# Two-layer graph block on one Trainium2 core: first layer as A(xW) in place of (Ax)W, its early sums stored as a finished node table

## Chip, core and metric

One core of a Trainium2 chip. The metric is device time in microseconds (us). The engines are TensorE (PE), VectorE (DVE), ScalarE (ACT), GpSimd (POOL) and SyncE (SP, which here only issues DMAs).

## What is computed

3125 nodes with 256 features each, 103125 edges sorted by destination (16 relation types). A is the matrix of edge counts with self loops, dinv the inverse root of the degree.

```python
def conv(h, W, b):
    h = h @ W
    agg = segment_sum(h[src] * norm, dst, num_segments=n)   # norm = dinv[src] * dinv[dst]
    return agg + b
h = relu(layernorm(x))
h = relu(conv(h, W1, b1)); h = relu(conv(h, W2, b2)); x = x + conv(h, W3, b3)
h = relu(layernorm(x))
red = segment_sum(h[src] + relvectors[edge_type], dst)       # without self loops
x = x + gru_cell(red, h, w_ih, w_hh, b_ih, b_hh)
```

## The kernel before

It never gathers rows. It first **builds** A as a dense f16 matrix of counts (`count`, 25 tiles of 128 sources by 3125 destinations), and then every layer is a chain of matmuls over it. All node tables are held as two f16 parts, high and low (the low part is the value minus the high part), so each product is two matmuls.

**The build** runs over 202 windows of 512 edges. For two windows at a time (a pair), DVE makes one-hot matrices (`one_hot`, L740, "hot"), into two buffers that take turns, and for pair m it waits until PE has done window 2m-3. PE multiplies them in a PSUM bank (L677, with small matmuls L682, L691, L693), ACT copies the window's 20 columns into `count` (L863). The banks form a ring of 6.

**Beats.** Each engine has four beats of side work per window, numbered 0, 1, 2, ... by constants (`VARIANCE_AT`, `DEGREE_AT`, ...). DVE does beats 8m to 8m+7 behind the one-hots of pair m, ACT beats 4s to 4s+3 behind its copy of window s, PE beats 4(s-1) to 4s-1 behind window s. Before the change they hold: the counts per rank for the degrees (L701, beats 0 to 19, PE), statistics of x (L441), degrees (L710, one burst behind window 9), the roots, and from beat 60 the table of the first layer: DVE shapes a tile of x (`L849`), ACT takes its high part (L873), DVE its low part (L840).

**Early products** (L731). From window 24 PE adds products of the first layer to every window, 1000 in all, each with a tile of the table stationary and 256 columns of `count` moving: `units` of 256 destinations that are already complete (`settled`), each in two halves of the features. They give (Ax) transposed for the first 2560 destinations. ACT copies each half out of PSUM (L882), SP stores it in DRAM (`table_scratch`). GpSimd adds the identity to the diagonal of each unit (L747).

**Behind the build** (`layers_pe`): SP loads the weights and the stored sums. PE makes the sums for the last 565 destinations (L915, 512 and 53 columns moving), and between them `conv_pe` (L929) multiplies the sums of all 25 tiles by W1, in f32. `scale_pe`, `scale_dve` and `scale_act` take the largest column sums of the weights, from which the powers of two that scale the f16 tables come. DVE (L1058, L1068, L1062) and ACT (L1133) make the table of the second layer, `node_b`, from the results. Then come layers 2 and 3 (700 products each), and the last with the GRU.

## Time and profile before

| | |
|---|---|
| median of 3 runs | 981.91 us (981.41 to 982.49) |
| the profiled execution | 982.03 us, of which its span 978.1 us |
| busy | PE 904.8 us, DVE 498.8, ACT 268.0, POOL 11.1 |
| matmuls on PE | 6312 |

The span is what lies between the first and the last instruction. Busy times overlap, since the engines run beside each other. PE is busy for 93% of the span, but it is so for different reasons in different stretches, so the stretches count and not the sum.

### The profile page before, as it was taken

The numbers are of one execution on the slowest core, as the hardware profiler recorded it, in microseconds if no ns is written. First come the engines' busy times: TensorE is split into PE (matmuls) and PEld (weight loads), VectorE is DVE, ScalarE is ACT, GpSimd is POOL, SyncE is SP. The second block draws the span as 40 slices with busy tenths as digits, with TensorE's granted clock in tenths as the row PEclk, the third lists the DMA queues.
The fourth block names the chain that finished last, engine by engine and source line by source line (L and its number), as shares of the span: only waits on it lengthen the run. The fifth ranks groups of instructions, "written<-read, shape, count | busy, mean of one in ns | idle before, by whom it ended". The sixth has DMA issues, their size and how long they took to land.

```text
span 978.1 us, 15791 instructions
## 1 busy us (share of the span) xinstructions
PE 904.8 (93%) x6312; PEld 557.3 (57%) x6312; DVE 498.8 (51%) x1300; ACT 268.0 (27%) x518; POOL 11.1 (1%) x18
## 2 busy tenths in 40 slices
PE   1654999999999798999999999999999999999996
PEld 1533888888888465544445454444455455555553
DVE  7999888888888164101112152333615133333435
ACT  3143444555544221101111120222322112122222
POOL 0000000000000000000000000000000000000000
PEclk9985999999999999999999999999999999999999
DMA  6000000000000400000000010111131000010010
GB/s 183 1 1 1 13 13 13 13 12 12 18 12 13 151 0 13 1 0 1 1 1 1 22 47 24 39 43 38 54 114 41 8 21 22 25 30 21 22 33 30
DMA packets 24502, 27.13 MB, mean 28 GB/s; under 512 B 2785, under 2 KB 22413, under 8 KB 24424
## 3 DMA queue, kind: packets, MB, share of 16 engines
q1 hardware_dynamic: 23752, 25.65, 8.3%
q8 instruction: 52, 0.85, 0.4%
q10 hardware_dynamic: 672, 0.41, 0.2%
q14 instruction: 26, 0.21, 0.1%
HBM read 17.03 MB, written 9.02 MB: 27 GB/s over the span
## 4 chain that ended last, share of the span: by engine, by line
PE 86%; DVE 10%; DMA 1%; ACT 1%; issue 1%; SPq 1%; DVEq 0%; ACTq 0%
PE ps L915 41%; PE ps L731 12%; PE ps L677 10%; PE ps L550 9%; PE ps L929 7%; PE ps L554 4%; DVE node_b L740 2%; DVE node_a L840 1%; PE ps L682 1%; DVE count L441 1%; PE ps L693 1%; DMA params<-in_L_gnn_b 1%; PE ps L535 1%; DVE count L797 1%; DVE agg L849 1%
## 5 line engine op out<-in xcount | busy, mean ns | idle before, releaser
L915 PE MATMUL ps<-count,node_b 128*128 128x512 f16 (+3 forms) x1400 | 271.3, 351 | 0.7 <-DVE node_b L1128 0.7
L740 DVE TENSOR_TENSOR node_b<-node_b 128x50 f16<-128x50 f16 (+4 forms) x455 | 208.6, 524 | 16.3 <-PE ps L677 16.3
L677 PE MATMUL ps<-node_b 128*128 128x225 f16 (+1 forms) x808 | 172.2, 298 | 35.5 <-DVE node_b L740 35.4
L915 PEld LDWEIGHTS ps<-count,node_b 128*128 128x128 f16 (+2 forms) x1400 | 121.4, 98 | 142.9 <-issue 8.4
L863 ACT ACTIVATE count<-ps 128x500 f32 x202 | 123.2, 610 | 164.6 <-PE ps L677 164.5
L915 PE MATMUL ps<-count,node_a 128*128 128x512 f16 (+1 forms) x900 | 162.6, 338 | 5.8 <-DMA params<-in_L_gnn_W 5.8
L731 PE MATMUL ps<-count,node_a 128*128 128x256 f16 (+1 forms) x1000 | 143.0, 274 | 0.0
L915 PEld LDWEIGHTS ps<-count,node_a 128*128 128x128 f16 x900 | 72.7, 98 | 93.2 <-issue 15.8
L677 PEld LDWEIGHTS ps<-node_b 128*128 128x128 f16 x808 | 83.1, 104 | 46.3 <-DVE node_b L740 34.4
L731 PEld LDWEIGHTS ps<-count,node_a 128*128 128x128 f16 (+1 forms) x1000 | 95.5, 98 | 20.8 <-issue 6.9
L682 PE MATMUL ps<-node_b,params 128*128 128x9 f16 (+1 forms) x808 | 104.7, 177 | 0.0
L1058 DVE SCALAR_TENSOR_TENSOR work<-ps,dinv,params 128x256 f32<-128x256 f32 (+1 forms) x50 | 24.0, 480 | 133.2 <-PE ps L929 110.5
L682 PEld LDWEIGHTS ps<-node_b,params 128*128 128x128 f16 x808 | 82.1, 102 | 11.1
L570 DVE TENSOR_TENSOR node_a<-ps,node_a 128x512 f32<-128x512 f32 (+1 forms) x25 | 17.2, 689 | 94.5 <-PE ps L550 94.5
L1137 ACT ACTIVATE agg<-ps,scales 128x512 f32<-128x512 f32 (+1 forms) x36 | 22.8, 638 | 120.4 <-PE ps L915 120.4
L929 PE MATMUL ps<-params,agg 128*128 128x256 f32 (+1 forms) x220 | 51.6, 386 | 4.2 <-ACT agg L1137 4.2
L1108 DVE SCALAR_TENSOR_TENSOR work<-ps,dinv,params 128x256 f32<-128x256 f32 (+1 forms) x25 | 12.1, 484 | 80.0 <-PE ps L929 79.3
L929 PEld LDWEIGHTS ps<-params,agg 128*128 128x128 f32 (+1 forms) x220 | 39.7, 186 | 14.9 <-ACT agg L1137 5.4
L550 PE MATMUL ps<-node_a 128*128 128x512 f32 (+1 forms) x100 | 47.0, 592 | 0.0
L512 ACT ACTIVATE node_a<-ps 128x256 f32<-128x256 f32 (+1 forms) x25 | 9.5, 378 | 125.3 <-PE ps L535 125.3
L693 PE MATMUL ps<-node_b 128*128 128x25 f16 x201 | 37.5, 186 | 0.0
L550 PE MATMUL ps<-node_a,agg 128*128 128x512 f32 x64 | 30.7, 601 | 2.6 <-issue 2.1
(195 smaller groups left out, 692.9 us busy)
## 6 DMA issues: line engine op xcount, KB each, us to landing
node_a<-in_x SPq DMA_DIRECT2D x4, 768.0 KB, 7.5
table_scratch<-agg SPq DMA_DIRECT2D x20, 128.0 KB, 1.8
node_b<-table_scratch SPq DMA_DIRECT2D x5, 512.0 KB, 8.6
xt<-x_scratch SPq DMA_DIRECT2D x16, 128.0 KB, 2.2
out<-scaled SPq DMA_DIRECT2D x16, 128.0 KB, 1.7
xt<-in_x SPq DMA_DIRECT2D x12, 128.0 KB, 2.1
params<-in_x SPq DMA_DIRECT2D x12, 128.0 KB, 2.1
x_scratch<-xt SPq DMA_DIRECT2D x12, 128.0 KB, 1.7
```

The lines of the kernel that those rows point to most:

```text
L550: done = PE.matmul(ps[0:m, rz, 0:2 * D], l, w[:, f, 0:2 * D], start=(n == 0), stop=(n == 2 * HALVES - 1))
L554: done = PE.matmul(ps[0:m, nn, col:col + D], ls[f], w[:, f, 2 * D:G], start=(f == 0), stop=(f == HALVES - 1))
L677: return PE.matmul(window(s)[:, :, first:first + n], low, key_hot[k][j // 2][:, j % 2, :, i].rearrange("p (t w) -> p t w", w=n), start=(s ...
L682: PE.matmul(ps[:, s % RING, last_tile + first:last_tile + first + n], rel_window(g, s % SMALL, j), span_hot[g][:, s % SMALL * QUARTERS // ...
L693: PE.matmul(window(s + 1)[:, :, 0], low, carry_hot[k][:, :, i], start=False, stop=False, skip_group_check=True)
L731: last = PE.matmul(ps[:, 6 + f, 0:UNIT], node_a[0:k, t, part, f * P:(f + 1) * P], count[0:k, t, u * UNIT:(u + 1) * UNIT], start=(t == 0 an ...
L740: return DVE.tensor_tensor(to, iota, keys.unsqueeze(2).to_broadcast([P, n, width, 2]), ALU.is_equal)
L863: ACTE.activation(to, window(s), ACT.Copy).then_inc(win_written, 1)
L915: last = PE.matmul(ps[:, b, 0:cols], nodes[0:k, t, part, f * P:(f + 1) * P], count[0:k, t, c * CHUNK:c * CHUNK + cols], start=(n == 0 and ...
L929: done = PE.matmul(ps[0:m, b, 0:D], sums[:, f, at_col:at_col + m], weight[i % 2][:, f, :], start=(f == 0), stop=(f == HALVES - 1))
L1058: DVE.scalar_tensor_tensor(out=work[k][0:m, :], in0=ps[0:m, 4 + (first + n) % 4, 0:D], scalar=dinv[0:m, t:t + 1], in1=bias[layer][0:m, :], ...
L1137: ACTE.activation(to[:, 0:cols], ps[:, h % AGG_RING, 0:cols], ACT.Copy, scale=inverse_scale).then_inc(sums_out, 1)
```

## The change

**The order of the first layer.** relu(layernorm(x)) W1 is made before the neighbours are summed. rstd is positive, so relu(rstd (x - mean)) is rstd relu(x - mean), and rstd is applied behind W1. GpSimd centres each tile of x as 2x minus twice its mean (L1333). PE turns the tile (two f32 transposes, one each beat from beat 8), ACT copies it back with Relu, PE multiplies it by W1 in f32 (three beats later), ACT copies that back over the tile (`beside_pe`, `beside_act`). There is one PSUM bank for the turned tile and one for the weighted one. From beat 58 ACT makes the high part of the table straight from it with the factor as scale (L1025), and DVE the low part from beat 68 (L905), so that DVE no longer shapes it. The table lies three tiles further down in the memory (`table0`), so ACT may write tile t only when DVE has made tile t-3.

**The early products** have the tile of `count` stationary and 256 features of the table moving: 128 destinations at once with all their features, 50 products for a tile of destinations, 21 tiles (1050 products). The first two are made together, 16 products a window from window 20, the other 950 from window 29 to the end. The result is the first layer's output itself. DVE adds the bias (L959), ACT does relu, scale and the high part (L967, L971), DVE the low part (L976), and SP stores the finished tile in DRAM, all during the build; four DMAs bring 21 tiles back to `node_b`.

**Moved and removed.** The scales are computed in the build (beats 37, 49 to 55). Behind the build PE makes 200 products of 256 columns for the last four tiles, with no `conv_pe` for the first layer, no `scale_pe` and no wait for the weights. The ring has 5 banks (L677 waits for `win_written` of one window less). GpSimd adds the diagonal by tiles of 128, 21 times.

```diff
-RING = 6
-EARLY = 5
+RING = 5
+EARLY = 21
+SHIFT = 3
...
+        TURN_AT = 8
+        WEIGH_AT = TURN_AT + 3
+        COLUMNS_AT = WEIGH_AT + T + 1
+        SCALE_AT = 49
+        FACTORS_AT = 58
+        LOW_PART_AT = FACTORS_AT + 10
+        OUT_AT, OUT_LOW_AT = 5, 9
...
+        PAIR_FROM = (LOW_PART_AT + 3) // BEATS + 3
+        REST_FROM = 29
+        early_products = [(u, t, part) for t in range(T) for u in range(2) for part in range(2)]
+        pair_products = len(early_products)
+        early_products += [(u, t, part) for u in range(2, EARLY) for t in range(T) for part in range(2)]
...
+        def beside_pe(beat):
...
+            t = beat - TURN_AT
+            if 0 <= t < T:
+                m = rows(t)
+                PE.wait_ge(x_centred, t + 1)
+                if t:
+                    PE.wait_ge(x_turned_out, t)
+                for f in range(HALVES):
+                    last = PE.transpose(TURNED[:, f, 0:m], h1[0:m, t, f * P:(f + 1) * P], ident[0:m, 0:m])
+                last.then_inc(x_turned, 1)
+            t = beat - WEIGH_AT
+            if 0 <= t < T:
+                m = rows(t)
+                PE.wait_ge(x_turned_out, t + 1)
+                PE.wait_ge(*((x_weighted_out, t) if t else (w_early_in[0], 16)))
+                for f in range(HALVES):
+                    last = PE.matmul(WEIGHED[0:m, :], turned_x(t)[:, f, 0:m], w_early[0][:, f, :], start=(f == 0), stop=(f == HALVES - 1))
+                last.then_inc(x_weighted, 1)
...
+            last = PE.matmul(out_slot(u)[0:m, :], count[0:k, t, u * P:u * P + m], table0(t)[0:k, part, :],
+                             start=(t == 0 and part == 0), stop=(t == T - 1 and part == 1), skip_group_check=True)
             if t == T - 1 and part == 1:
-                last.then_inc(early_summed, 1)
+                last.then_inc(conv_done, 1)
...
+        def out_bias_dve(u):
+            m, k = rows(u), u % 2
+            DVE.wait_ge(conv_done, u + 1)
...
+            DVE.scalar_tensor_tensor(out=work[k][0:m, :], in0=out_slot(u)[0:m, :], scalar=newt[0:m, 1, u:u + 1], in1=xt[1][0:m, :],
+                                     op0=ALU.mult, op1=ALU.add).then_inc(conv_read, 1)
...
+            t = beat - TURN_AT
+            if 0 <= t < T:
+                m = rows(t)
+                ACTE.wait_ge(x_turned, t + 1)
+                ACTE.activation(turned_x(t)[:, :, 0:m], TURNED[:, :, 0:m], ACT.Relu).then_inc(x_turned_out, 1)
+            t = beat - WEIGH_AT
+            if 0 <= t < T:
+                m = rows(t)
+                ACTE.wait_ge(x_weighted, t + 1)
+                ACTE.activation(h1[0:m, t, :], WEIGHED[0:m, :], ACT.Copy).then_inc(x_weighted_out, 1)
...
         def fast_pool():
+            for t in range(T):
+                m = rows(t)
+                POOL.wait_ge(x_summed, min(t // 6, XG) + 1)
+                POOL.tensor_scalar(h1[0:m, t, :], h1[0:m, t, :], 2.0, moments[0:m, t, 0:1], ALU.mult, ALU.subtract).then_inc(x_centred, 1)
```

PE's instructions at the end of window 4, where two of its four beats can be seen. L701 (L738 after) are the counts per rank, L749 the transposes, L757 the product with W1, "waits" are the semaphores. Before:

```order
L693 MATMUL ps<-node_b 128x25
L677 MATMUL ps<-node_b 128x25x11
L701 MATMUL ps<-ones,count 128x1 [waits ranks_ready]
L701 MATMUL ps<-ones,count 128x1 x3
L701 MATMUL ps<-ones,count 74x1 x4
```

Now:

```order
L697 MATMUL ps<-node_b 128x25x11
L738 MATMUL ps<-ones,count 128x1 [waits ranks_ready]
L738 MATMUL ps<-ones,count 128x1 x3
L738 MATMUL ps<-ones,count 74x1 x4
L749 MATMUL ps<-ident,node_a 128x128 [waits x_turned_out,x_centred]
L749 MATMUL ps<-ident,node_a 128x128
L757 MATMUL ps<-count,node_a 128x256 [waits x_weighted_out,x_turned_out]
L757 MATMUL ps<-count,node_a 128x256
```

Each beat from 11 to 32 has a transpose pair and a product pair on PE now, and both wait for a copy by ACT.

PE's instructions where the build ends: the last early products (L731, now L779), and what follows. Before:

```order
L731 MATMUL ps<-count,node_a 128x256 x5
L915 MATMUL ps<-count,node_a 128x512 [waits w0_in,w1_in,chunk_looped,win_written]
L915 MATMUL ps<-count,node_a 128x512 x25
L938 MATMUL ps<-agg,xt 128x256 [waits abs_made]
L938 MATMUL ps<-agg,xt 128x256 x3
L915 MATMUL ps<-count,node_a 128x512 x12
L929 MATMUL ps<-params,node_b 128x256 [waits early_in0]
```

Now:

```order
L779 MATMUL ps<-node_a,count 128x256 x5
L1095 MATMUL ps<-scaled,count 128x256 [waits conv_read,chunk_looped,win_written]
L1095 MATMUL ps<-scaled,count 128x256 x3
L1095 MATMUL ps<-xt,count 128x256 x2
L1095 MATMUL ps<-node_a,count 128x256 x44
L1095 MATMUL ps<-scaled,count 128x256 [waits conv_read]
```

The waits for the weights and the stored sums are gone from this place, and so are L938 and L929.

DVE's instructions between the one-hots of two pairs (windows 18 and 19) in the table's stretch. Before:

```order
L740 TENSOR_TENSOR node_b<-node_b 128x1100
L840 SCALAR_TENSOR_TENSOR node_a<-scaled,node_a 128x256 [waits table_high]
L849 TENSOR_SCALAR scaled<-node_a,newt 128x256 [waits table_ready]
L840 SCALAR_TENSOR_TENSOR node_a<-scaled,node_a 128x256 [waits table_high]
L849 TENSOR_SCALAR scaled<-node_a,newt 128x256 [waits table_ready]
L840 SCALAR_TENSOR_TENSOR node_a<-work,node_a 128x256 [waits table_high]
L849 TENSOR_SCALAR work<-node_a,newt 128x256 [waits table_ready]
```

Now:

```order
L788 TENSOR_TENSOR node_b<-node_b 128x50
L788 TENSOR_TENSOR node_b<-node_b 128x1100
L905 SCALAR_TENSOR_TENSOR node_a<-node_a,newt 128x256 [waits table_high] x8
L788 TENSOR_TENSOR params<-node_b 128x8x32 [waits win_done]
L788 TENSOR_TENSOR node_b<-node_b 128x1024
```

Of the two operations for a tile one is left, in runs of eight.

## Rows read from the trace of the kernel before

**Rows 1.** Windows: stretch, length, busy us of PE, PEld, DVE, ACT, POOL; PEclk; DMA

```profile
24.00:60.50 36.50, 24.78 (x336) 19.95 (x335) 35.77 (x108) 9.14 (x16) 0.00 (x0) 1.00 0.01 2
60.50:92.50 32.00, 11.90 (x109) 7.73 (x108) 31.14 (x86) 15.04 (x37) 0.67 (x1) 0.56 0.00 1
92.50:322.30 229.80, 229.74 (x2778) 195.22 (x2776) 191.03 (x439) 113.39 (x198) 7.91 (x9) 0.99 0.04 13
322.30:381.80 59.50, 50.32 (x309) 32.72 (x310) 30.83 (x87) 13.71 (x35) 0.38 (x1) 0.97 0.20 63
```

**Rows 2.** Timeline of ACT (start, us): copies of windows 10, 11, 13, 14 and 28

```profile
57.87 0.59 ACT L863 ACTIVATE count<-ps 128x500 f32 x1 [2.75 <-PE ps L677]
58.97 0.60 ACT L863 ACTIVATE count<-ps 128x500 f32 x1 [0.51 <-PE ps L677]
61.22 0.60 ACT L863 ACTIVATE count<-ps 128x500 f32 x1 [0.17 <-PE ps L677]
62.01 0.59 ACT L863 ACTIVATE count<-ps 128x500 f32 x1 [0.19 <-PE ps L677]
...
99.55 0.59 ACT L863 ACTIVATE count<-ps 128x500 f32 x1 [0.71 <-PE ps L677]
```

**Rows 3.** Timeline of PE: the rank counts behind window 3, the start of window 10

```profile
35.27 1.77 PE L701 MATMUL ps<-ones,count 128*128 128x1 f16 x32
56.47 0.39 PE L677 MATMUL ps<-node_b 128*128 128x225 f16 x1 [1.00 <-DVE node_b L740]
```

**Rows 4.** Timeline in the GRU: a transpose pair, the next matmul, ACT's copy

```profile
817.22 0.38 PE L535 MATMUL ps<-ident,scaled 128*128 128x128 f32 x2
817.44 1.89 PE L915 MATMUL ps<-count,node_b 128*128 128x512 f16 x8
817.64 0.38 ACT L512 ACTIVATE node_a<-ps 128x256 f32<-128x256 f32 x1 [4.14 <-PE ps L535]
```

**Rows 5.** Timeline behind the build: four tiles by W1, the next matmul, DVE

```profile
340.37 3.62 PE L929 MATMUL ps<-params,node_b 128*128 128x256 f32 x16
343.82 2.86 PE L915 MATMUL ps<-count,node_a 128*128 128x512 f16 x12
344.09 0.48 DVE L1058 SCALAR_TENSOR_TENSOR work<-ps,dinv,params 128x256 f32<-128x256 f32 x1 [2.20 <-PE ps L929]
```

**Rows 6.** Timeline: a copy by ACT and the PE matmul that waits for it

```profile
373.83 0.58 ACT L1137 ACTIVATE agg<-ps 128x512 f32<-128x512 f32 x1
374.46 3.72 PE L929 MATMUL ps<-params,agg 128*128 128x256 f32 x16 [1.41 <-ACT agg L1137]
```

**Rows 7.** Timeline of ACT: the load of the table for Sqrt

```profile
49.39 1.28 ACT L421 ACT_TABLE_LOAD   x1
```

**Rows 8.** Timeline: one-hots beside a GpSimd operation, the operation, one-hots alone

```profile
108.43 2.60 DVE L740 TENSOR_TENSOR node_b<-node_b 128x176 f16<-128x176 f16 x5 [0.32 <-PE ps L677]
109.18 1.17 POOL L747 TENSOR_TENSOR count<-count,ident 128x256 f16<-128x256 f16 x1 [33.70 <-ACT count L863]
113.52 2.13 DVE L740 TENSOR_TENSOR node_b<-node_b 128x176 f16<-128x176 f16 x5 [0.32 <-PE ps L677]
```

**Rows 9.** Timeline of DVE: two low parts with a shape between, three low parts

```profile
68.13 0.42 DVE L840 SCALAR_TENSOR_TENSOR node_a<-agg,node_a 128x256 f16<-128x256 f32 x1
68.91 0.42 DVE L840 SCALAR_TENSOR_TENSOR node_a<-agg,node_a 128x256 f16<-128x256 f32 x1
85.25 1.08 DVE L840 SCALAR_TENSOR_TENSOR node_a<-agg,node_a 128x256 f16<-128x256 f32 x3
```

**Rows 10.** Chain that ended last: one small dependent operation of a root

```profile
61.27 0.20 DVE count L427
```

**Rows 11.** Timeline of PE: products in window 199, window 200's start, behind the build

```profile
318.99 0.71 PE L731 MATMUL ps<-count,node_a 128*128 128x256 f16 x5
319.54 0.27 PE L677 MATMUL ps<-node_b 128*128 128x225 f16 x1
328.05 7.07 PE L915 MATMUL ps<-count,node_a 128*128 128x512 f16 x26 [5.81 <-DMA params<-in_L_gnn_W]
```

More of the change, by code:

```diff
@@ L30 @@
 LOADS = 4
-SCALE1 = float(2 ** 11)
 class Count:
@@ L305, in settled @@
         def settled(u):
-            return UNIT_FIRST + UNIT_STEP * u
-        assert all(settled(u) * N > (u + 1) * UNIT * FULL for u in range(UNITS))
+            return SETTLE_FIRST + SETTLE_STEP * (u // 2) + SETTLE_ODD * (u % 2)
+        assert all(settled(u) * N > (u + 1) * P * FULL for u in range(SETTLES)) and settled(SETTLES - 1) < NS
         def prepare_dve():
@@ L441, in x_stats_dve, with x_sums_dve @@
             DVE.bn_stats(x_raw[0:m, t, :], h1[0:m, t, :]).then_inc(x_stats, 1)
+        def x_sums_dve(first, end):
+            DVE.wait_ge(x_stats, end)
+            DVE.tensor_tensor(moments[:, first:end, 0], x_raw[:, first:end, 1], x_raw[:, first:end, 4], ALU.add).then_inc(x_summed, 1)
         def x_variance_dve():
@@ L711, in build_pe @@
                                              high_of[0:lanes(q), (q * WINDOW + w) // 2, :, w % 2],
-                                             start=(w == 0 and q == 0), stop=(w == WINDOW - 1 and q == Q - 1))
+                                             start=(w == 0 and q == 0), stop=(w == WINDOW - 1 and q == Q - 1), skip_group_check=True)
                     last.then_inc(degrees_done, 1)
-                for issued in range(issued, products_after[s]):
-                    early_product_pe(issued)
+                for u, t, part in early_products[issued:products_after[s]]:
+                    early_product_pe(u, t, part)
@@ L864, in build_act @@
                 for beat in range(BEATS * s, BEATS * (s + 1)):
-                    if beat == VARIANCE_AT - AHEAD_ACT:
-                        x_root_act()
-                    if beat == DEGREE_AT - AHEAD_ACT:
-                        inverse_root_act(degree[:, 3, :], [degree[:, i, :] for i in range(3)])
-                    t = beat - SHAPE_AT
-                    if 0 <= t < T:
-                        m = rows(t)
-                        ACTE.wait_ge(table_shaped, t + 1)
-                        ACTE.activation(node_a[0:m, t, 0, :], spare[t % len(spare)][0:m, :], ACT.Relu).then_inc(table_high, 1)
@@ L900, in program @@
+            for g, (first, end) in enumerate(RELOADS):
+                SP.dma_start(node_b[:, first:end, :, :].rearrange("p t a d -> p t (a d)"), early_dram(first, end)).then_inc(early_in[g], 16)
+            for i in (1, 0):
+                SP.dma_start(weight[i], convs[i or 2][0].rearrange("(f p) d -> p f d", p=P)).then_inc(w_in[i or 2], 16)
+            for i in (1, 2):
+                SP.dma_start(bias[i], spread(convs[i][1])).then_inc(biases_in, 16)
         H_LAYER = HALVES * NC
@@ L931, in conv_pe, with first_ready @@
             done.then_inc(conv_done, 1)
[L933 to L939 removed]
+        def first_ready(t):
+            return (early_in[t // 6], 16) if t < EARLY else (node_ready, t + 1)
         def nothing(n):
@@ L989, in between @@
                             gru_pe(h0, due.pop(0))
-                    sums_pe(h0 + HALVES * i + f, node_b, c, f, REL_ROW + R, (lambda t: 2 * T + place[t] + 1) if i == 0 and f == 0 else None, between)
+                    sums_pe(h0 + HALVES * i + f, node_b, c, f, REL_ROW + R, (lambda t: (node_ready, 2 * T + place[t] + 1)) if i == 0 and f == 0 else None, between)
                     if due:
```

450 lines of the change are left out of this document (230 added, 220 removed).

## Prediction

> **What bounds the kernel now.** I read the windows view by stage first, then the timelines of single engines inside a stage, because the engine that waits changes three times.
>
> From 24 to 60.5 us and from 60.5 to 92.5 us DVE is busy 35.77 of 36.50 and 31.14 of 32.00 us, PE 24.78 and 11.90 [rows 1]: the first 24 windows are as fast as DVE can make one-hots and do its beats. From 92.5 to 322.3 PE is busy all the time and DVE 191.03 of 229.80 us: windows 24 to 201 are as fast as PE. From 322.3 to 381.8 the first layer is finished (59.5 us), with PE the longest part of it but not all. The rest, from 381.8 to 978.1, is PE in layers that the change leaves alone: 596.3 us, taken over as they are.
>
> One thing must be seen in the clock. The column says 1.00 up to 60.5 us, yet windows 10 and 11 follow each other by 1.10 us (57.87, 58.97) and windows 13 and 14 by 0.79 [rows 2]. The first is TensorE at the lower level, 1.2 GHz; it rose near 61 us, after PE had worked without a break from 56.5 [rows 3]. So I price PE's early work at the lower level until it has been busy for a few us. At the higher level a window's own matmuls take what is left of a steady window: (322.3 - 99.4) us over 173 windows [rows 1, 2] is 1.29 us, less 5.6 products of 0.11 us (5 in 0.55 us, from 318.99 to 319.54 [rows 11]), so 0.67 us, small stalls included; I take 0.65.
>
> **The change part by part.**
>
> *Windows 3 to 10, new work on PE.* Per tile of x two f32 transposes, 0.22 us (817.22 to 817.44 [rows 4]), and a product with W1, 3.45 us for four tiles (340.37 to 343.82 [rows 5]), 0.86 us each; 0.43 and 1.72 at the lower level. That is 1.08 us of work for each of 25 beats. But there is one bank for the weighted tile. When the product of one beat ends, ACT starts 0.20 us later (817.44 to 817.64 [rows 4]), copies for 0.38, and PE follows 0.05 behind (373.83 + 0.58 to 374.46 [rows 6]): 0.63 us, of which the transposes between cover 0.22. So a beat takes 0.63 + 0.86 = 1.49 us at the higher level, and 2.35 at the lower (with the rank counts, 1.65/4 = 0.4 us a beat [rows 3], 0.4 + 0.43 + 1.72 = 2.55). The other end for the handshake is none, 1.08 us; I take the full one, since both copies stand in ACT's queue in the same order. The sum: window 3 (four counts and transposes in a chain of 1.07, one product) 1.1 + 0.8 + 3.2 + 1.7 = 6.8; window 4 two beats at the lower and two at the higher level, 1.1 + 5.1 + 3.0 = 9.2; window 5 0.65 + 4 x 1.49 = 6.6; windows 6 to 8 the same with 0.4 less for the first beat, 6.2 each; window 9 the same and 40 small degree matmuls, taken at their 1.3 us, 7.5; window 10 and four products of weights 0.65 + 1.7 = 2.4. In window 7 ACT also loads the Sqrt table, 1.28 us [rows 7], of which some 0.9 is not covered. In all 52.0 us. Before, PE went from window 3 (34.2, since 1.06 us of window stand ahead of 35.27) to window 11 (1.1 behind 56.47 [rows 3]), 23.4 us, with DVE the bound. **+28.6 us.** DVE's side of it is hidden now: it waits for PE.
>
> *GpSimd's centring* (25 operations, 128x256 f32). Nothing here has this form; a two-input one of 128x256 f16 takes 1.17 us beside one-hots, and stretches a set of them from 2.13 to 2.60 [rows 8]. Below 1.49 us it keeps ahead of PE. The first six tiles fall on the one-hots of windows 2 and 3, when DVE is still the bound: between 0 and 5 x 0.47 = 2.4 us; I take **+2.0**, near the top, because each of the five large one-hots can meet one. The Trainium skill (SBUF, State Buffer, section "Who interferes with whom") says that a GpSimd operation and a DVE operation with two SBUF inputs exclude each other for the full instruction. By it the six would cost six whole operations, about 7 us if each held the port for 1.17 us; the row has 0.47 us for one of 1.17, and I go by the row.
>
> *Windows 11 to 28.* DVE waits for the weights' column sums, then: a reduction and seven small steps (about 0.2 us each [rows 10]) 2.0 us, the root and factors 2.0, low parts at 0.33 to 0.42 us a tile in place of 0.78 for low part and shape (68.13 to 68.91, three in 1.08 [rows 9]), so 1.5 and 3.2 us for 4 and 8 tiles, and one-hots of 2.1 [rows 8] for four pairs: 2.2 + 2.1 + 2.0 + 2.1 + 1.5 + 2.1 + 3.2 + 2.1 = 17.3 us to window 20. From there PE is the bound with 16 products a window: 0.65 + 1.76 = 2.41; window 20 at the lower level at first, 4.2; five more 12.0; windows 26 to 28 2.4. In all 35.9 us. Before: from 57.6 to the end of window 28's products, 0.6 behind the start of its copy's input at 99.4 [rows 2], 100.0, so 42.4. **-6.5 us.** The ping-pong between DVE and ACT over three table tiles is 0.42 + 0.42 + 0.1 us for three tiles, less than DVE's own work. It is hidden.
>
> *Windows 29 to 201.* 5.49 products in place of 5.62: 173 x 0.13 x 0.11 = **-2.4 us.** DVE gets a bias and a low part for 21 tiles, 0.48 [rows 5] + 0.42 us = 19 us. Its cover: DVE is idle 38.8 us in that stage [rows 1], 0.4 us a pair; and one-hots may be late by another 0.7 us before PE waits, since DVE starts them 3.1 us ahead of their use and needs 2.4. GpSimd's 21 additions and ACT's two extra copies a tile fit too. The ring of 5 asks for a copy four windows back. All nothing; uncovered, DVE's part is 19 us.
>
> *The end of the build.* Before: 59.5 us. It has 5.8 us for the weights, and the first 26 products in 7.07 us [rows 11], which at 0.22 each would be 5.7. Now PE's last product is followed by 0.20 + bias 0.48 + relu 0.4 + high part 0.4 + low part 0.42 + the diagonal 0.5 and hops of 0.05: 2.65 us, and then 200 products of 256 columns at 0.11 and four changes of tile, 22.8 us. **25.5 in place of 59.5: -34.0 us.** The finished tiles come back meanwhile: four DMAs of 2.7 MB, issued some 4.5 us behind the build (the chain above and the last store). Before, the first stored sums were multiplied at 340.4 [rows 5], 18 us behind the build and with weights and biases ahead of them; now the second layer asks after 25 us. I take no wait; the bound on the other side is a rival below. Of the new steps on SP, the weights stand behind these four and are asked for a chunk later.
>
> Sum: 28.6 + 2.0 - 6.5 - 2.4 - 34.0 = -12.3 us. The span 978.1 becomes 965.8. The profiled execution lies 3.93 us above its span and 0.12 above the median, so **969.6 us**, 1.3% below the median of 981.91.
>
> **The rivals.**
>
> *TensorE stays at the lower level through windows 3 to 10.* For it: it did so to 61 us with PE busy 24.78 of 36.50, and the new stretch has gaps of 0.2 to 0.4 us in every beat. Against: it rose after 4.4 us without a break, and PE now works 2.15 of each 2.35 us. Each of 22 beats that I priced at the higher level costs 0.86 more, each of seven windows 0.45: 22 us, so **991.6 us, slower**. It decides from 13 such beats on. The Trainium skill (TensorE: Matmul & The Clock Gate, section "PE-mode transpose") says that transposes do not count as PE being busy in the same way. By it the 0.43 us of transposes is taken off, 1.72 of 2.35 us counts, and this rival gains; no row here separates them.
>
> *GpSimd is slower than a beat.* If a centring takes 2.0 us, nearly twice the longest row, 24 x 0.5 = 12 us more: 982, no change. For it: DVE's one-hots stand in its way. Against: DVE idles in this stretch.
>
> *DVE's bias and low parts are not hidden*, say a third of 19 us: 976; all of it: 989.
>
> *The handshake is hidden after all*: 22 x 0.41 = 9 us less, 960.5. For it only that the copy may overlap the end of the product; the rows of the GRU speak against it.
>
> *The saved tail turns into a wait for the reload.* The four DMAs would have to take more than 21 us, where before all weights and the first of five were through 18 us behind the build. A wait of 5 us would still leave 974.6. Small.
>
> **How the numbers follow.** The forecast as worked out, 965 to 975, 0.50; no handshake 0.12; lower clock 0.14; slow GpSimd 0.08; DVE not hidden 0.08; anything else 0.08, to both sides. A measurement tells changes over 0.2%, 2 us. Faster: 0.50 + 0.12 and half of the last three, 0.12, and the part of the clock rival with fewer than 13 beats, 0.02: 0.76. Same 0.05, slower 0.19. The range goes down to the case without handshake and a little past it, 959, and up past the slow GpSimd, 985; it leaves out the clock rival in full and DVE unhidden in full.
>
> **What would show it.** In the profile after: windows 3 to 9 at 6 to 9 us each, PE's products with W1 1.5 us apart, each waiting for ACT, and DVE idle with PE as releaser; window 11 near 88 us; window 29 near 124; the last early product near 344; the second layer's first product near 369.5, 25.5 us later. The prediction is wrong if the transposes and W1 products come more than 2 us apart for long, if PE waits for one-hots behind window 30, or if the second layer waits for its tiles.

## The result and the profile after

The changed kernel takes 969.95 us (median of 4 runs, 968.96 to 970.29), the kernel before in the same comparison 982.2 us (981.41 to 983.98, 4 runs). The ratio is 0.9871, 95% interval 0.9854 to 0.9888: 1.3% faster. The profiled span is 966.0 us, the forecast 965.8 for the span and 969.6 for the time.

So close a hit calls for a look at its parts. Windows view of the kernel after, in the forecast's stages: up to window 3, windows 3 to 10, 11 to 28, 29 to 201, the end of the build, and the rest from the second layer's first product on. Columns: stretch, length, busy us of PE, PEld, DVE, ACT, POOL, PEclk, DMA share, GB/s.

```profile
0.00:32.85 32.85, 10.97 (x131) 9.12 (x132) 27.47 (x133) 11.98 (x14) 7.43 (x11) 1.00 0.53 156
32.85:86.53 53.68, 47.95 (x377) 37.44 (x377) 25.14 (x74) 23.68 (x60) 30.82 (x24) 1.00 0.00 1
86.53:122.87 36.34, 27.67 (x282) 21.76 (x281) 31.09 (x85) 19.93 (x43) 0.80 (x1) 0.77 0.00 1
122.87:343.40 220.53, 219.81 (x2680) 187.12 (x2677) 199.68 (x469) 120.47 (x215) 12.49 (x19) 1.00 0.04 14
343.40:370.29 26.89, 24.45 (x202) 20.24 (x201) 3.38 (x9) 3.88 (x9) 0.00 (x0) 0.94 0.43 138
370.29:966.00 595.71, 583.90 (x2751) 298.11 (x2750) 191.96 (x497) 108.25 (x228) 0.00 (x0) 1.00 0.09 26
```

| stage | before | forecast | measured | miss |
|---|---|---|---|---|
| to window 3 | 34.2 | 36.2 | 32.85 | -3.35 |
| windows 3 to 10 | 23.4 | 52.0 | 53.68 | +1.7 |
| windows 11 to 28 | 42.4 | 35.9 | 36.34 | +0.4 |
| windows 29 to 201 | 222.3 | 219.9 | 220.53 | +0.6 |
| end of the build | 59.5 | 25.5 | 26.89 | +1.4 |
| the rest | 596.3 | 596.3 | 595.71 | -0.6 |

The five forecasts behind the first are right to 6% or better, the first is off by 9%. The misses sum to +0.2 us because a gain that nobody forecast in the first stage pays for small losses behind it. The stages also change roles as forecast: in windows 3 to 10 PE is busy 47.95 of 53.68 us and DVE only 25.14, the reverse of [rows 1].

Inside windows 3 to 10, timeline of PE and ACT. Window 5, a beat with rank counts (L738), transposes (L749) and product (L757), and ACT's two copies; then window 6, without counts:

```profile
52.20 0.54 PE L738 MATMUL ps<-ones,count 128*128 128x1 f16 x8
52.40 0.38 ACT L1013 ACTIVATE node_a<-ps 128x256 f32<-128x256 f32 x1 [0.63 <-PE ps L757]
52.60 0.42 PE L749 MATMUL ps<-ident,node_a 128*128 128x128 f32 x2
52.93 1.10 PE L757 MATMUL ps<-count,node_a 128*128 128x256 f32 x4
53.87 0.54 PE L738 MATMUL ps<-ones,count 128*128 128x1 f16 x8
54.07 0.38 ACT L1013 ACTIVATE node_a<-ps 128x256 f32<-128x256 f32 x1 [0.63 <-PE ps L757]
...
57.99 1.10 PE L757 MATMUL ps<-count,node_a 128*128 128x256 f32 x4 [0.30 <-ACT node_a L1013]
58.93 0.38 PE L749 MATMUL ps<-ident,node_a 128*128 128x128 f32 x2
59.13 0.38 ACT L1013 ACTIVATE node_a<-ps 128x256 f32<-128x256 f32 x1 [1.01 <-PE ps L757]
59.66 1.10 PE L757 MATMUL ps<-count,node_a 128*128 128x256 f32 x4 [0.35 <-ACT node_a L1013]
```

Both kinds of beat take 1.67 us (52.20 to 53.87, 57.99 to 59.66), not the 1.49 forecast. In both the chain is the forecast's: ACT starts 0.20 us behind the product (53.87 to 54.07, 58.93 to 59.13), its copy takes 0.38, then comes PE's next product. But PE comes 0.15 behind the copy in place of 0.05 (52.40 + 0.38 to 52.93, 59.13 + 0.38 to 59.66), and the product holds PE 0.94 us in place of 0.86: 0.94 + 0.20 + 0.38 + 0.15 = 1.67. In the first kind no wait is printed: counts (0.40) and transposes keep PE busy in the record until the product starts (0.33 later). The sum says that the chain sets this beat too, and the first experiment bears it out. By windows, 3 to 10 took 7.3, 8.2, 7.2, 6.7, 7.1, 6.7, 8.0 and 2.4 us, where the forecast had 6.8, 9.2, 6.6, 6.2, 7.1, 6.2, 7.5 and 2.4.

The end of the build, timeline:

```profile
343.56 0.48 DVE L959 SCALAR_TENSOR_TENSOR work<-ps,newt,xt 128x256 f32<-128x256 f32 x1 [3.14 <-PE ps L779]
344.08 0.51 ACT L967 ACTIVATE agg<-work,dscale 128x256 f32<-128x256 f32 x1 [0.49 <-DVE work L959]
344.62 0.42 ACT L971 ACTIVATE agg<-agg 128x256 f16<-128x256 f32 x1
345.06 0.43 DVE L976 TENSOR_TENSOR agg<-agg 128x256 f16<-128x256 f32 x1 [1.02 <-ACT agg L971]
345.41 0.35 DVE L795 TENSOR_TENSOR count<-count,ident 128x384 f16<-128x384 f16 x1
...
345.95 0.60 PE L1095 MATMUL ps<-scaled,count 128*128 128x256 f16 x4 [2.44 <-issue]
...
346.60 6.74 PE L1095 MATMUL ps<-node_a,count 128*128 128x256 f16 x44
...
353.94 5.07 PE L1095 MATMUL ps<-node_a,count 128*128 128x256 f16 x44
```

The forecast's chain stands there link by link: bias, relu, high part, low part, diagonal, and PE 2.55 us behind the end of the last product (forecast 2.65). What it had not seen are the 44 products in 6.74 us where the same 44 take 5.07 a tile later. The granted clock says why: it is 0.50, the lower level, from 346.6 to 350.0 us. PE had been idle for 2.44 us and had worked again for some 0.65 us (from 345.95) when the clock fell.

```profile
346.60:350.00 3.40, 3.40 (x19) 2.41 (x17) 0.00 (x0) 0.00 (x0) 0.00 (x0) 0.50 0.35 88
350.20:353.00 2.80, 2.80 (x27) 2.32 (x26) 0.00 (x0) 0.00 (x0) 0.00 (x0) 1.00 1.09 369
```

The second layer begins at 370.29 and does not wait for its tiles.

GpSimd's 25 operations, from the view of line L1333 (count, shortest/median/longest in ns, first and last start):

```profile
L1333 POOL TENSOR_SCALAR node_a<-node_a,moments x25: 1137/1152/3244, 27.5 to 61.6; 128x256 f32<-128x256 f32 x24, 53x256 f32<-53x256 f32 x1
```

### The profile page after: what moved, and what is told of

The parts are those of the page before. It is cut to its first block, busy times and chain, and to the rows that moved or that the text cites. A ratio compares the mean times of both kernels' runs of the same rounds, so it can differ in the third digit from the quotient of the medians.

```text
span 966.0 us, 16081 instructions
## 1 busy us (share of the span) xinstructions
PE 914.8 (95%) x6412; PEld 573.8 (59%) x6412; DVE 478.7 (50%) x1264; ACT 288.2 (30%) x567; POOL 51.5 (5%) x54
## 4 chain that ended last, share of the span: by engine, by line
PE 90%; DVE 6%; ACT 2%; issue 1%; DMA 0%; SPq 0%; DVEq 0%; ACTq 0%
PE ps L1064 40%; PE ps L779 12%; PE ps L697 11%; PE ps L547 9%; PE ps L1075 4%; PE ps L551 4%; PE ps L757 3%; PE ps L1095 3%; DVE node_b L788 2%; PE ps L702 1%; PE ps L713 1%; PE ps L749 1%; PE ps L532 1%; PE ps L738 1%; ACT node_a L1013 0%
## 5 line engine op out<-in xcount | busy, mean ns | idle before, releaser
L697 PE MATMUL ps<-node_b 128*128 128x225 f16 (+1 forms) x808 | 167.3, 291 | 16.2 <-DVE node_b L788 16.2
L1064 PE MATMUL ps<-count,node_a 128*128 128x512 f16 (+3 forms) x700 | 135.4, 352 | 0.0
L779 PE MATMUL ps<-node_a,count 128*128 128x256 f16 (+1 forms) x924 | 131.7, 273 | 0.0
L1064 PEld LDWEIGHTS ps<-count,node_a 128*128 128x128 f16 (+1 forms) x700 | 59.9, 97 | 74.2 <-issue 7.2
L702 PE MATMUL ps<-node_b,params 128*128 128x9 f16 (+1 forms) x808 | 102.4, 175 | 0.0
L779 PEld LDWEIGHTS ps<-node_a,count 128*128 128x128 f16 (+1 forms) x924 | 88.8, 98 | 16.7 <-issue 4.3
L1156 DVE SCALAR_TENSOR_TENSOR work<-ps,dinv,params 128x256 f32<-128x256 f32 (+1 forms) x25 | 12.0, 480 | 125.3 <-PE ps L1075 125.3
L1235 ACT ACTIVATE agg<-ps,scales 128x512 f32<-128x512 f32 (+1 forms) x36 | 22.8, 638 | 119.9 <-PE ps L1064 119.9
L1206 DVE SCALAR_TENSOR_TENSOR work<-ps,dinv,params 128x256 f32<-128x256 f32 (+1 forms) x25 | 12.1, 484 | 79.6 <-PE ps L1075 78.6
L1075 PE MATMUL ps<-params,agg 128*128 128x256 f32 (+1 forms) x200 | 46.8, 386 | 1.6 <-ACT agg L1235 1.6
L1075 PEld LDWEIGHTS ps<-params,agg 128*128 128x128 f32 (+1 forms) x200 | 36.3, 187 | 11.6 <-issue 4.2
L1333 POOL TENSOR_SCALAR node_a<-node_a,moments 128x256 f32<-128x256 f32 (+1 forms) x25 | 35.2, 1424 | 23.0 <-DVE moments L442 23.0
```

The lines of the kernel that those rows point to most:

```text
L697: return PE.matmul(window(s)[:, :, first:first + n], low, key_hot[k][j // 2][:, j % 2, :, i].rearrange("p (t w) -> p t w", w=n), start=(s ...
L702: PE.matmul(ps[:, s % RING, last_tile + first:last_tile + first + n], rel_window(g, s % SMALL, j), span_hot[g][:, s % SMALL * QUARTERS // ...
L779: last = PE.matmul(out_slot(u)[0:m, :], count[0:k, t, u * P:u * P + m], table0(t)[0:k, part, :], start=(t == 0 and part == 0), stop=(t == ...
L1064: last = PE.matmul(ps[:, b, 0:cols], nodes[0:k, t, part, f * P:(f + 1) * P], count[0:k, t, c * CHUNK:c * CHUNK + cols], start=(n == 0 and ...
L1075: done = PE.matmul(ps[0:m, b, 0:D], sums[:, f, at_col:at_col + m], weight[i % 2][:, f, :], start=(f == 0), stop=(f == HALVES - 1))
L1333: POOL.tensor_scalar(h1[0:m, t, :], h1[0:m, t, :], 2.0, moments[0:m, t, 0:1], ALU.mult, ALU.subtract).then_inc(x_centred, 1)
```

## The experiments

The theory with which the runs were planned: (1) windows 3 to 10 are set by PE's own work in the beats with counts, and by the handshake with ACT over one bank in the others; (2) GpSimd's centring costs DVE nothing; (3) the end is a chain on DVE and ACT plus a clock that falls; (4) DVE's new work in the steady stage is hidden. Times are medians of 4 runs, each against the kernel before in the same comparison (982.75 to 982.88 us there, 982.2 in the changed kernel's own, so a difference against the changed kernel can be 0.6 us too small).

### Two banks in turn for the weighted tile

```diff
-RING = 5
+RING = 4
...
-                PE.wait_ge(*((x_weighted_out, t) if t else (w_early_in[0], 16)))
+                PE.wait_ge(*((x_weighted_out, t - 1) if t > 1 else (w_early_in[0], 16)))
...
-                    last = PE.matmul(WEIGHED[0:m, :], ...
+                    last = PE.matmul(WEIGHED[t % 2][0:m, :], ...
```

> Two PSUM banks take turns for the weighted tile (the ring of windows gives one up, 4 in place of 5), so PE waits for the copy of two tiles back. Theory: in the beats with rank counts (0 to 19) the beat of 1.67 us is PE's own work, counts 0.40, transposes 0.33, product 0.94, and the copy is hidden; the handshake costs only in beats 20 to 35, where PE idles 0.30 to 0.57 us a beat, some 5.1 us in all. So window 11 starts 5 us earlier, DVE has room for it, and the time is about 965. Rival A: behind the copy GpSimd is next (1.41 us for a tile on the mean), and less than 2 us is saved. Rival B: the handshake costs in all 22 full-clock beats, as the prediction had it, 9 us. Rival C: the ring of 4 makes PE wait for copies in the steady stage, and the gain is lost.

Measured 963.04 us (962.62 to 963.42), ratio 0.98 (0.9784 to 0.9816): 6.9 us less than the changed kernel (the profiled executions differ by 7.5), more than the 5.1 us of idle time. Timeline of PE in this run, windows 5 and 6:

```profile
51.40 0.54 PE L738 MATMUL ps<-ones,count 128*128 128x1 f16 x8
51.80 0.42 PE L749 MATMUL ps<-ident,node_a 128*128 128x128 f32 x2
52.05 1.03 PE L757 MATMUL ps<-count,node_a 128*128 128x256 f32 x4
52.91 0.54 PE L738 MATMUL ps<-ones,count 128*128 128x1 f16 x8
...
57.30 0.38 PE L749 MATMUL ps<-ident,node_a 128*128 128x128 f32 x2
57.52 1.03 PE L757 MATMUL ps<-count,node_a 128*128 128x256 f32 x4
58.38 0.38 PE L749 MATMUL ps<-ident,node_a 128*128 128x128 f32 x2
```

A beat without counts is now 1.08 us (57.30 to 58.38), transposes 0.22 and product 0.86: exactly the forecast's prices of the bare work. A beat with counts is 1.51 (51.40 to 52.91), not 1.67, so the theory is wrong there: the handshake set that beat too, and hid in places where no wait is printed. A beat without counts gained 0.59 us: 0.35 of printed idle time, 0.16 of the transposes' end, which now overlaps the product (0.38 us long, 0.22 from start to start), and 0.08 in the product. A beat with counts gained 0.16: from the transposes' start to the product's it is 0.25 in place of 0.33, and the product is again 0.08 shorter. The rows of the stationary loads (PEld) show where these 0.08 come from. The changed kernel, then two banks:

```profile
57.96 0.73 PEld L757 LDWEIGHTS ps<-count,node_a 128*128 128x128 f32 x4 [0.51 <-issue]
```

```profile
57.41 0.73 PEld L757 LDWEIGHTS ps<-count,node_a 128*128 128x128 f32 x4
```

Where PE waits for ACT, the load waits too, and begins 0.03 us ahead of its product (57.96, 57.99); with two banks it begins 0.11 ahead (57.41, 57.52), beside the transposes. Windows 3 to 10 take 46.11 us in place of 53.68:

```profile
32.98:79.09 46.11, 44.23 (x376) 36.83 (x376) 25.15 (x74) 23.71 (x60) 30.76 (x24) 1.00 0.01 1
```

Half of the 7.6 us is idle time (PE 1.9 us not busy in place of 5.7), the other half PE's busy time, 44.23 in place of 47.95, by the parts above; 0.3 us of it is not the edit's, since window 4's first product was still partly at the lower level in the changed kernel (1.19 us to the next start, 0.86 here). Rivals A and C fall: the next wait (1.29 us once, for ACT) is ACT's table load in window 7, and the smaller ring costs nothing that shows. Rival B has the mechanism right, the handshake in every beat, and the size too large: 9 us for 7.6.

### The diagonal ahead of tile 20's bias and low part

```diff
+                if m == PAIRS - 1:
+                    DVE.wait_ge(win_written, NS)
+                    loops(ALU.add, EARLY).then_inc(chunk_looped, 1)
                 for s in range(s0, s0 + 2):
...
-            DVE.wait_ge(win_written, NS)
-            loops(ALU.add, EARLY).then_inc(chunk_looped, 1)
```

> DVE adds the diagonal of the last tiles as soon as ACT has copied the last window, ahead of the bias and low part of tile 20, instead of behind them. Theory: PE's first product behind the build comes about 1.7 us earlier (344.2 in place of 345.95), and with an idle time of 0.8 us in place of 2.44 the clock stays up, so that the first 50 products take 5.7 us in place of 7.3: 3.3 us in all, about 966.6. Rival: the clock falls anyway and 1.7 us is saved, 968.2. Rival: the finished tile 20 now comes late, the reload starts later and the second layer waits: no change.

Measured 967.55 us (966.91 to 967.87), ratio 0.9843 (0.9826 to 0.9859). Timeline of PE; the last early products start at 344.14 here:

```profile
344.14 0.81 PE L779 MATMUL ps<-node_a,count 128*128 128x256 f16 x5
...
345.61 0.60 PE L1096 MATMUL ps<-scaled,count 128*128 128x256 f16 x4 [0.66 <-ACT count L990]
346.04 0.38 PE L1096 MATMUL ps<-xt,count 128*128 128x256 f16 x2
346.26 5.07 PE L1096 MATMUL ps<-node_a,count 128*128 128x256 f16 x44
...
368.28 4.06 PE L1065 MATMUL ps<-count,node_b 128*128 128x512 f16 x18
```

Idle 0.66 us in place of 2.44, the first 44 products in 5.07 us, and from the last early products' start to the second layer 24.1 us in place of 27.6 (342.70 to 370.29): 3.4 us, as the theory had it, at a granted clock of 1.00. The time fell by 2.4 only. In this execution the last early products come 1.4 us later than in the changed kernel's, 1.3 of it in windows 20 and 21, where the granted clock rose from 0.50 to 1.00 near 110.6 us here and near 107.7 us there.

Tile 20, now later, is not missed, so the second rival falls. But that the shorter idle time kept the clock up is not shown. The other runs can be laid beside it, since all have this place:

| executions | idle time of PE | first 50 products |
|---|---|---|
| the changed kernel; two banks | 2.44, 2.43 us | 7.32, 7.32 us |
| without product; without centring; the two with a slower GpSimd | 2.43 each | 5.65 to 5.66 |
| bias and low part doubled | 3.41 | 7.32 |
| this run; the four below that have its edit | 0.65 to 0.66 | 5.65 to 5.66 |

One of the four in the second row, GpSimd with the cheap second operation:

```profile
348.46 0.60 PE L1095 MATMUL ps<-scaled,count 128*128 128x256 f16 x4 [2.43 <-issue]
348.89 0.38 PE L1095 MATMUL ps<-xt,count 128*128 128x256 f16 x2
349.11 5.07 PE L1095 MATMUL ps<-node_a,count 128*128 128x256 f16 x44
```

Behind 2.43 us the clock fell in two of six profiled executions, behind 0.65 us in none of five. So the edit is worth 1.8 us by its earlier start, and the other 1.67 only in an execution in which the clock would have fallen. An estimate: 1.8 + 1.67 x 2/6 = 2.3 us, close to the 2.4 measured. Whether the shorter idle time excludes the fall stays open with five executions.

### No transposes, no product; then no centring either

The first leaves out `beside_pe`'s transposes and product and ACT's two copies; the second also GpSimd's loop. The edit deletes those lines and replaces the waits that hung on them. The table is then not that of the reference.

> Leaves out the transposes, the relu of x, the product with W1 and ACT's two copies; GpSimd still centres x. The table is made of the centred x, so the output is not the reference's. Theory: windows 3 to 10 go back to DVE's pace, 23.4 us as before the change in place of 53.7, and nothing of it is given back later: 940 us. GpSimd now works beside a DVE that is the bound; as the one-hots of 27.95 (2.12 us) and 35.14 (1.97 us) were not stretched by it, this costs less than 1 us. Rival: each of the 25 operations stretches a set of one-hots by the 0.47 us that the profile of before showed for one, 5 to 11 us: 945 to 951. Rival: the work on PE was partly hidden under DVE, and 945 or more remains for that reason; then windows 3 to 10 take longer than 23.4 us with DVE waiting.

> As the run without transposes and product, and without GpSimd's centring too (output not the reference's). Theory: the same time as that run within 1 us, since DVE keeps its pace and GpSimd is what waits. Rival: 5 to 11 us less, by the 0.47 us for each operation.

Measured 952.47 us (952.15 to 952.83) and 943.35 us (942.3 to 944.27). The theory is wrong twice: the first run should have been 940, and the two should have been alike. They differ by 9.1 us, so with DVE as the bound the centring is not free. Where does it go? Timelines of DVE in the first of the two runs, one-hots of pair 3 and the scales:

```profile
54.29 2.32 DVE L771 TENSOR_TENSOR node_b<-node_b 128x176 f16<-128x176 f16 x5
...
69.72 0.16 DVE L909 SCALAR_TENSOR_TENSOR bounds<-fours 128x1 f32<-128x1 f32 x1 [7.62 <-POOL fours L1309]
```

and the same pair in the second:

```profile
53.33 2.13 DVE L771 TENSOR_TENSOR node_b<-node_b 128x176 f16<-128x176 f16 x5
```

The rival named the one-hots, and they account for about 1 us: the first six sets sum to 13.24 us beside GpSimd and 12.24 without. 7.6 us are another thing: the scales wait for GpSimd's reduction over partitions, which stands behind the 25 operations in GpSimd's queue and starts at 69.3 us in place of 49.2. In the changed kernel DVE asks for it only after window 11 began, near 87.5 us, so there this wait does not exist. The second run is still 3.4 us above the 940 expected: its windows 3 to 10 take 26.3 us, not 23.4, in part because the column sums of the weights now stand in them, for which DVE waits 1.8 us. Against that run the changed kernel pays 26.6 us (969.95 - 943.35) for transposes, product and centring; the forecast's terms for windows 3 to 10 and the centring were 28.6 + 2.0.

### GpSimd made slower: a cheap second operation, and the centring twice

```diff
+                POOL.tensor_scalar(h1[0:m, t, :], h1[0:m, t, :], 1.0, 0.0, ALU.mult, ALU.add).then_inc(x_same, 1)
+                POOL.wait_ge(x_same, t + 1)
```

> GpSimd does a second operation of the same shape on each tile of x (times 1 plus 0, in place), so that a tile costs it some 2.5 us in place of 1.41. Theory: GpSimd had only 0.25 us a tile to spare against PE's beat of 1.67, so it becomes the bound of windows 3 to 10: it ends at about 27.5 + 25 x 2.5 = 90 us in place of 62.8, and the last tile needs some 6 us of PE behind it, so window 11 comes near 97 in place of 86.5. The reduction over partitions that stands behind it in GpSimd's queue comes at 96, which costs no more on top. In all 8 to 12 us more: 978 to 982, the change's whole gain. Rival: GpSimd's operations were stretched to 1.41 by DVE and not by themselves, and the second one is short: under 4 us more.

Measured 971.83 us (970.99 to 972.59), 1.9 more, as its rival had it. It does not decide: the second operation took 0.41 us where nothing stood in its way, so that a tile took 1.62 us, still under PE's beat; PE waited for GpSimd six times, 2.2 us in all. Hence the other form, in which the added operation has the centring's own operands and writes a buffer that is not used:

> The changed kernel, in which GpSimd does each centring twice (first into a buffer that is not used). The copy tried before took it 0.41 us and left it at 1.62 us a tile, just under PE's beat of 1.67, and cost 1.9 us. Theory: now 2.4 us a tile, GpSimd becomes the bound: the last tile is centred near 27.5 + 25 x 2.4 = 88 us in place of 62.8, window 11 comes near 95 in place of 86.5, and the reduction over partitions behind it near 94, when DVE needs it at 88.7: 8 to 10 us more, 978 to 980, most of the gain. Rival: PE's queue of windows covers it, under 4 us.

Measured 988.05 us (986.6 to 988.38), ratio 1.0054 (1.0037 to 1.0071): slower than before the change. Timeline of GpSimd, and a wait of PE:

```profile
34.85 3.12 POOL L1335 TENSOR_SCALAR node_a<-node_a,moments 128x256 f32<-128x256 f32 x1
...
88.15 1.14 POOL L1335 TENSOR_SCALAR node_a<-node_a,moments 128x256 f32<-128x256 f32 x1
89.27 1.14 POOL L1333 TENSOR_SCALAR work<-node_a,moments 128x256 f32<-128x256 f32 x1
...
91.71 0.44 PE L749 MATMUL ps<-ident,node_a 128*128 128x128 f32 x2 [1.06 <-POOL node_a L1335]
```

GpSimd needs (94.0 - 27.2)/25 = 2.67 us a tile, PE waits for it, and window 11 starts at 103.72 in place of 86.53. The direction is the theory's, the size is not: 18 us for an expected 8 to 10. A tile cost more than the 2.4 assumed (6.8 us over 25), PE had 9.7 us to do behind the last tile, not 7, and the clock was at its lower level for part of the time in which PE waited (a mean granted clock of 0.66 from 50 to 60 us, and of 0.83 from 70 to 80 and from 80 to 90). The forecast's rival of a slow GpSimd, priced at 12 us for 2.0 us a tile, was no small danger: GpSimd took 1.41 us a tile (35.24 us for 25), 0.26 below PE's beat.

### DVE's new work in the steady stage doubled

```diff
             DVE.scalar_tensor_tensor(out=work[k][0:m, :], in0=out_slot(u)[0:m, :], ...).then_inc(*dve_seq.up())
+            DVE.wait_ge(*dve_seq.now)
+            DVE.scalar_tensor_tensor(out=work[k][0:m, :], in0=out_slot(u)[0:m, :], ...).then_inc(conv_read, 1)
```

and the same for the low part.

> DVE does the bias and the low part of the first 21 finished tiles twice, 21 x (0.48 + 0.43) = 19 us more work in the build, with the same results. DVE is idle 20.8 us of the 220.5 us of the steady stage. Theory (the prediction's): idle time of DVE there covers such work, under 1 us more, 970 to 971. Rival: a third of such work falls on pairs whose one-hots PE then waits for, 6 us more, 976. If this holds, part of what the change gave DVE once is on the path too.

Measured 973.37 us (971.83 to 974.31), 3.4 more: between theory and rival. From tile 2's first product to the last group of early products it takes 220.51 us in place of 218.45, 2.1 more for 19 us of DVE's work. PE's waits there:

```profile
129.63 0.28 PE L697 MATMUL ps<-node_b 128*128 128x225 f16 x1 [1.20 <-DVE node_b L788]
135.33 0.28 PE L697 MATMUL ps<-node_b 128*128 128x225 f16 x1 [0.55 <-DVE node_b L788]
```

They stand at the start, where the first two tiles are finished together. The changed kernel itself has one such wait of 0.15 us in the whole stage. Another 1.0 us comes behind it: tile 20's bias and low part stand in the chain at the end of the build, and PE's idle time there is 3.41 us in place of 2.44. This execution also entered the stage 0.9 us late; it is 3.8 us above the changed kernel's profiled one. So the first 19 us were covered, and a second 19 us are nearly so.

### The table ten beats earlier

```diff
-        COLUMNS_AT = WEIGH_AT + T + 1
-        WEIGHT_AT = 34
-        DEGREE_AT = 46
-        SCALE_AT = 49
-        FACTORS_AT = 58
+        COLUMNS_AT = 14
+        WEIGHT_AT = 27
+        DEGREE_AT = 38
+        SCALE_BEATS = [24, 41, 42, 43, 44, 45, 46]
+        FACTORS_AT = 48
...
```

> The two edits measured before (two banks for the weighted tile, here from tile 13 on; the diagonal first at the end of the build), and the scales, degrees and factors made some ten beats earlier: the column sums of the weights at beat 14 in the spare bank, the degrees at beat 38, the factors at beat 48, the first low part at beat 58. The work is the same. Theory: in windows 11 to 19 DVE is the bound (31.1 of 36.3 us to window 29) while it is idle for over half of windows 3 to 10; 4 us of scales, factors and some 4 us of low parts leave windows 11 to 19, PE idles 3 us there in place of 8.7. Window 11 to window 29 takes 31 us in place of 36.3. With 963.0 for two banks and 3.0 for the diagonal, 955. Rival: DVE waits in windows 8 to 10 for the degrees or for GpSimd's reduction (which lands at 69 us), its one-hots come late, and nothing is gained by the third edit: 960.

Measured 965.86 us (964.62 to 966.53): worse than two banks alone, and outside both the theory (955) and the rival (960). PE's products still waited for window 20, so DVE's low parts were early for nobody, and up to tile 12 the single bank was back (the spare one held the column sums). PE still idled for one-hots, 2.82, 2.73, 3.17 and 3.44 us at four places between 84 and 103 us. That these were the causes is argued from the program; the last run below, which mends both, is the test.

### The kernel before, once more

> The kernel before the change once more, for its first 25 us. In the profile of before, GpSimd made the identity at 9.67 us and the first window was copied at 25.27; in all profiles of the changed kernel and of its variants the identity came at about 2.6 and the first window at 23.8 to 24.5. If the 1.5 us belong to the execution and not to the kernel, this profile can show 2.6 and 24; if they belong to the kernel, 9.7 and 25.3 again.

One run, 983.82 us. Timeline of GpSimd in it, and of GpSimd in the run with the centring once and a copy:

```profile
9.61 0.28 POOL L272 TENSOR_SCALAR_AFFINE_SELECT ident<-ident 128x128 f32<-128x128 f32 x1 [9.17 <-issue]
```

```profile
2.61 0.29 POOL L267 TENSOR_SCALAR_AFFINE_SELECT ident<-ident 128x128 f32<-128x128 f32 x1 [2.17 <-DVE ident L309]
```

The first window is copied at 25.22 us (25.27 in the profile of before that the forecast used), and at 23.5 to 24.5 in the changed kernel and its variants. So some 0.7 to 1.8 us of the gain belong to the program and not to the execution. Why GpSimd starts its identity 7 us earlier there stays open.

### What gained, put together

> The two edits that gained alone, together: two banks in turn for the weighted tile (963.0 alone) and the diagonal first at the end of the build (967.6 alone, second layer begun 3.4 us earlier behind the last early product). They lie 250 us apart and share nothing. Theory: they add, 963.0 - 3.4 = 959.6. Rival: the run with the third edit, 965.9, shows that they don't add, and this gives over 962.

Measured 960.65 us (959.96 to 960.79), ratio 0.9775. The two edits add: the single runs gained 6.9 and 2.4 us, which gives 960.6. The 959.6 expected had counted the diagonal's 3.4 us of one execution.

The products of the first two tiles in another order, on top of both:

```diff
+        PAIR_STEPS = [8, 0, 16, 8, 8, 10, 9, 9, 8, 8, 8, 8]
+        PAIR_FROM = 17
...
-        early_products = [(u, t, part) for t in range(T) for u in range(2) for part in range(2)]
+        early_products = [(u, t, part) for u in range(2) for t in range(T) for part in range(2)]
```

> The two edits together, and only the order of the first 100 products changed: those of destination tile 0 first, behind windows 17, 19 and on, as far as their low parts are made, instead of both tiles together from window 20 at 16 a window. No work is moved on DVE or ACT. Theory: with two banks, window 20 began at 97.0 us and window 29 at 116.3, 19.3 us at PE's pace of 2.39 a window, while PE idled 8.7 us from window 12 to 20. 24 products go where PE idles, so windows 20 to 28 fall to DVE's pace, some 15.4 us: 3.7 us less, 956. Rival: the products then wait for low parts one by one and hold up windows 18 and 20, and nothing is gained: 959.6.

Measured 958.13 us (957.24 to 958.71), ratio 0.975; the second layer starts at 357.71 us in place of 360.02. The edit works, at 2.3 to 2.5 us for the expected 3.7.

> The version with the early table (965.9), with two of its faults mended: two banks already from tile 5 on (the column sums of the weights at beat 12, DVE's reduction at beat 17), and the 100 products of the first two tiles of destinations spread from window 15 on, those of one destination tile first, behind odd windows, where PE idled 2.7 to 3.4 us for one-hots. Theory: that version lost 4.7 us to the single bank up to tile 12 and could not use its early low parts, since the products waited for window 20. Now DVE alone sets windows 11 to 28: 955. Rival: DVE's waits for the roots of ACT hold the one-hots up, and it stays at 960 or more.

Measured 956.83 us (955.27 to 959.39), ratio 0.9744 (0.9726 to 0.9762). Windows view from window 11 to window 29, the changed kernel's stretch of 36.34 us:

```profile
78.59:112.18 33.59, 27.09 (x283) 20.44 (x280) 31.60 (x81) 22.27 (x48) 2.20 (x3) 0.90 0.02 5
```

The stretch starts 7.9 us earlier and is 2.7 us shorter. DVE is busy 31.60 of 33.59 us in it, so it is now nearly all DVE's, as the theory had it. The version without moved DVE work takes 35.5 us for it (79.28 to 114.79). In the times the lead over that version is 1.3 us and lies within their ranges. It is the fastest version found, 2.6% below the kernel before and 1.35% below the changed one.

## Why the prediction was right, step by step

**The end of the build, -34.0 forecast, -32.6 measured.** Its two parts hold: the chain (2.65 forecast, 2.55 measured) and 200 products at 0.11 us. The step that was too small is "200 products of 256 columns at 0.11 and four changes of tile, 22.8 us": the first 50 ran partly at the lower clock, 7.3 us in place of 5.7. This is a matter of the execution: in four others with the same 2.43 us of idle time the 50 took 5.65 us, and there the forecast's 22.8 is met. The rows of before held the hint: the first 26 products behind an idle time of 5.81 us took 7.07 us [rows 11], and the forecast priced those rightly and gave its own no such risk.

**Windows 3 to 10, +28.6 forecast, +30.3 measured.** The beat of 1.49 was in truth 1.67. That shows as 0.5 us too little in each of windows 5, 6, 8 and 9, and in window 3 at the lower level; in window 7 the Sqrt load took it back (the window is 0.4 us longer than window 6, where 0.9 was priced). Against it, the clock rose one beat earlier than forecast, in window 4, which was 1.0 us shorter. The case without handshake was priced at 9 us, 0.41 for each of 22 beats; the second bank, which makes it true, gained 7.6 in the stage and 6.9 in the time. By the forecast's own prices six of these beats, those with counts, had nothing to gain (0.40 + 1.08 = 1.48 us of work in a beat of 1.49), which leaves 16 x 0.41 = 6.6 us. What the forecast had no step for are the 0.10 us more between copy and product and the 0.08 by which a wait uncovers the load of f32 weights.

**GpSimd's centring, +2.0 forecast, nothing measured.** DVE's one-hots of windows 2 and 4 take 2.12 and 1.97 us in the changed kernel, 2.11 and 1.96 in the run without GpSimd's work, though a GpSimd operation met each of them. The wait fell on the other side: GpSimd's operation of 1.15 us takes up to 3.24 when it meets a set. By the Trainium skill (SBUF — State Buffer, section "Who interferes with whom") such a meeting is an exclusive lock, in which "issue order, not op shape, decides who blocks". The rows agree with the lock: the 3.12 us above are 1.14 and the 1.97 us of the set that it met. They add that the wait lasted through the set's four instructions, not through one. DVE pays now and then too, 0.2 us on two later sets in the changed kernel and 0.2 to 0.4 on four in the run without product. It costs the changed kernel nothing, because DVE has time there.

**Windows 11 to 28, -6.5 forecast, -6.1 measured**, with DVE's order of scales, factors and low parts as written. **The steady stage, -2.4 forecast, -1.8 measured**, with DVE's 19 us covered: PE waits once for one-hots, 0.15 us.

**The clock rival** (991.6 us) did not come. Timeline of PE: the transposes take 0.67 us a pair at 41.73 and 0.41 at 43.78, so PE reached the higher level in window 4 and held it through gaps of 0.35 us in each beat. The Trainium skill's remark that transposes do not count as PE being busy in the same way (TensorE: Matmul & The Clock Gate, section "PE-mode transpose") can't be tested by this, since products or counts stood beside them throughout.

**What was not foreseen** is the preparation, 1.35 us shorter to window 3. With the unneeded +2.0 it makes the 3.35 us that cover the other misses. Without this luck the forecast would have been some 3.5 us low, still inside its range. That the total came within 0.4 us is luck; that five of the six stages came within 6% is not.

## What to carry to other kernels

When work moves onto an engine and hands its results to another over one buffer, price the beat as the full round trip, and price the second buffer at once: here it was worth 7 us beside a change worth 12, and more than the idle time that the trace printed. A beat without a printed wait can still be set by the handshake: add up the round trip before calling it the engine's own work. Give work to an idle engine only with its spare time per unit in hand (GpSimd had 0.26 us a tile), and see what stands behind it in its queue. A short stall in front of dense matmul work can cost more than its length, since the clock may fall behind it; put what the matmuls wait for first in the other engines' queues. And before a difference of clock between two executions is put down to an edit, look at the same place in all the others.

## What the hardware showed unexpectedly

- PE at the lower level for 3.4 us from 346.6 us on, behind an idle time of 2.44 us and after PE had resumed; the same idle time left the clock at 1.00 in four of six executions.
- An f32 product of 256 columns, two passes of features, takes PE 0.94 us when its stationary load has to wait for ACT and 0.86 when not. A pair of f32 transposes takes 0.22 us from start to start.
- GpSimd's tensor_scalar on 128x256 f32: 1.14 us with an operand per partition (times 2, less the operand), 0.41 us with constants alone (times 1 plus 0), both in place. Which of the differences does it was not separated.
